# A one-core attention and expert block: route columns carried through the projection, residual by turns of x, expert weights stationary, all orders written anew

## The chip, the cores and the metric

The kernel runs on one core of a Trainium2 chip. The metric is the device time of one execution in microseconds (us). The core's engines run programs of their own and meet at semaphores: TensorE (PE) does matmuls into PSUM, VectorE (DVE) and ScalarE (ACT) do element work, GpSimd (POOL) does element work and issues the indirect DMAs, SyncE (SP) issues plain DMAs.

## What is computed

The input x has 4096 rows (4 sequences of 1024) of 128 features.

```python
x = x + attn(layernorm(x))
x = x + ffn(layernorm(x))
# attn: q, k, v = h @ W + b in 16 heads of 8; q and k normalised in each head
#       out = ((q @ k.T) / n ** sigmoid(m)) @ v ; out @ Wo + bo      (no softmax: linear)
# ffn:  logits = h @ router_w.T ; the best of 16 experts, score = sigmoid(top logit)
#       routed = (up * silu(gate)) @ down, with gate_up of the expert on h * score
#       shared = (silu(h @ sg.T) * (h @ su.T)) @ sd.T                (512 wide)
#       return shared + routed
```

Attention has no softmax, so for each sequence keys and values fold into one 128 x 128 matrix (keys times v, masked by head), which is multiplied by Wo and then applied to q.

## The kernel before, in words

**Tiling.** Rows are handled in 32 tiles of 128, four tiles to a chunk: eight chunks c = 0..7 of 512 rows. Two chunks are one sequence. Everything is float32; a float32 matmul is issued as two TensorE instructions. The shared expert's gate and up products are the exception: the operands are split into a high and a low part in float32r (`hT_hi` on ACT, `hT_lo` on POOL for the activations), and three float32r matmuls make one product.

**Stage one, attention, by chunk.** `x_stats` (L721, L724: four `bn_stats` and four `bn_aggr`), `std_x` and `x_scales` make the row scale. `project` (L1096) multiplies the columns of x (`xT`) by centred weights `w_c` into 384 columns: q, k and v. `take` (L758) scales them, adds the bias and writes `qkv` (two buffers). `square`, `head_sums` (L766), `head_norms`, `inv_norms` (L771) make the norms of the heads; POOL's `scale_v` and `scale_q` (L319) apply them. `v_by_k` (L1105) makes the 128 x 128 matrix of a sequence, `mask_vk` masks it, `fold_wo` (L1114) multiplies by Wo, `turn_q` transposes q. `attend` makes the residual in PSUM: the bias as a float32r product of 512 columns (L1129), x times the identity of 512 columns (L1130), then q times the folded matrix (L1135).

**Stage two, routing, by chunk.** ACT copies the sum out (`x1_copy`), DVE takes its statistics (`x1_stats`), `norm_h` writes `h_rows`, `turn_h` transposes them, `route` (L1152) multiplies by the router, and `choose` and `place` (ten small DVE instructions on PSUM) find each row's expert and its position `pos` in `x_slots`, a DRAM table with a region for each expert. POOL's `scatter(t)` (L345) sends one tile by an indirect DMA; it waits for the scatter two before it.

**Stage three, experts.** When all counts are known, `slot_rows` and `take_table` write a table of row numbers and expert numbers for 48 slots of 128 rows, in 12 groups of four. SP waits for all 32 scatters and loads group after group (`load`, L248: four row numbers read into registers by a TENSOR_LOAD, then four DMAs). For a group: `turn_rows` (L1215) transposes, `rows_copy` (L528), `gate_up_experts` (L1226: the rows stationary, 256 weight columns moving, the weights' address from a register), `gate` and `gated` (the score applied as a scale, one instruction per tile), `turn_act` (L1234, transposes again), `turned_act` (L877), `down_experts` (L1245), `take_y` (L545), and POOL's `send` (L354): an indirect DMA per slot into `y_back`, waiting for the send three before it.

**Stage four.** When all 48 sends have landed, SP brings `y_back` home in eight DMAs; `add_shared` and `add_experts` add, and eight DMAs write the output.

**The shared expert** is the filler. `gate_up_shared(n)` (six float32r matmuls of 512 columns, L1181 to L1183), `silu_shared(n)`, `act_shared(n)`, `down_shared(n)` (L1203) for n = 0..31, four for a chunk, stand between the other pieces in each engine's list.

**Order.** There is no scheduler: each engine's order is a written list of such calls, and an engine does the next call only when the one before has been issued. Before the first `turn_rows` TensorE does 10 of the 32 `gate_up_shared`; ACT's `score_tanh(g)` reads the score column of the loaded group g and so waits for its load.

## Time and profile before

| | us |
|---|---|
| median of 3 runs | 213.24 (212.55 to 214.74) |
| the profiled execution, whole | 212.35 |
| its span in the profile | 210.6 |
| TensorE busy | 185.7 (88%) |
| VectorE busy | 137.5 (65%) |
| GpSimd busy | 111.8 (53%) |
| ScalarE busy | 103.1 (49%) |

Times are counted from the span's start. The whole execution is 1.75 us longer than its span. TensorE's granted clock is 0.997 of full over the execution. The matmuls are pipelined, so the durations of a row overlap those of the next by some 0.15 us; the distance from start to start is what an instruction takes on the engine.

### The profile page before, as it was taken

The page shows a single profiled execution, that of the slowest core. Times are in us where ns is not written, and L with a number is a line of the kernel's source. Part 1 is how long each engine was busy: PE and PEld are TensorE (multiplying, and loading weights), DVE is VectorE, ACT ScalarE, POOL GpSimd, SP SyncE. Part 2 cuts the span into 40 slices and gives each one's busy share as a digit, 9 for nine tenths or more (in the row PEclk, how much of TensorE's full clock was granted, in tenths as well). Part 3 has the DMA queues.
Part 4 walks back from the last instruction along what each step waited for, and adds up shares of the span by engine and source line. Part 5 has one row for each costly group of instructions (what it writes and reads, how often), then busy time and mean ns, then how long its engine had stood idle before and what let it go on. Part 6 is the DMA issues. An engine that isn't in the chain of part 4 may idle for free.

```text
span 210.6 us, 3716 instructions
## 1 busy us (share of the span) xinstructions
PE 185.7 (88%) x1110; PEld 152.0 (72%) x1110; DVE 137.5 (65%) x430; ACT 103.1 (49%) x234; POOL 111.8 (53%) x142
## 2 busy tenths in 40 slices
PE   0797698988989699889779999999999999979992
PEld 0344566766668477778568999889999889869882
DVE  4789999999999979667443455454545233237553
ACT  3434474967564798943323666565634322312320
POOL 7003405348779786757800177767777767750000
PEclk9999999999999999999999999999999999999998
DMA  6999993001100011111134456511111100048143
GB/s 171 302 390 269 174 413 134 2 0 38 40 30 25 26 38 41 51 40 51 41 85 106 114 136 154 143 43 43 42 40 38 50 31 0 0 135 311 56 165 133
DMA packets 17606, 21.58 MB, mean 102 GB/s; under 512 B 3224, under 2 KB 11679, under 8 KB 17332
## 3 DMA queue, kind: packets, MB, share of 16 engines
q1 hardware_dynamic: 13872, 15.73, 26.3%
q0 software_dynamic: 2560, 4.24, 6.1%
q10 hardware_dynamic: 1156, 1.39, 1.9%
q8 instruction: 9, 0.15, 0.3%
q14 instruction: 9, 0.07, 0.1%
HBM read 13.95 MB, written 8.44 MB: 106 GB/s over the span
## 4 chain that ended last, share of the span: by engine, by line
PE 35%; DVE 31%; DMA 12%; POOL 10%; issue 8%; ACT 2%; POOLq 1%; ACTq 0%; DVEq 0%
PE quad_banks L1226 8%; DVE qkv L758 7%; DMA y_back<-yg,xg 7%; PE bank L1203 7%; POOL y_back L354 7%; DVE ss L766 4%; DVE st L721 4%; PE quad_banks L1181 3%; PE bank L1245 3%; PE quad_banks L1183 3%; PE quad_banks L1182 3%; DMA x_slots<-h_rows,pos 3%; POOL x_slots L345 2%; PE bank L1215 2%; PE quad_banks L1096 2%
## 5 line engine op out<-in xcount | busy, mean ns | idle before, releaser
L354 POOL DMA_INDIRECT y_back<-yg,xg x48 | 47.0, 979 | 30.9 <-ACT yg L545 15.2
L843 DVE TENSOR_TENSOR s_act<-quad_banks,sg_act 128x512 f32<-128x512 f32 x32 | 22.1, 689 | 28.9 <-PE bank L1203 16.6
L517 ACT ACTIVATE sg_act<-quad_banks 128x512 f32<-128x512 f32 x32 | 19.1, 598 | 44.5 <-PE quad_banks L1183 44.4
L345 POOL DMA_INDIRECT x_slots<-h_rows,pos x32 | 31.6, 988 | 11.8 <-issue 6.9
L1203 PEld LDWEIGHTS bank<-sdT,s_act 128*128 128x128 f32 x256 | 31.8, 191 | 1.8
L1203 PE MATMUL bank<-sdT,s_act 128*128 128x128 f32 x256 | 32.8, 276 | 0.0
L319 POOL TENSOR_TENSOR qkv<-qkv,rn 128x512 f32<-128x512 f32 x16 | 17.1, 1081 | 26.6 <-DVE rn L771 26.5
L1096 PE MATMUL quad_banks<-w_c,xT 128*128 128x384 f32 x64 | 25.0, 525 | 2.1 <-DVE qkv L758 1.3
L1226 PE MATMUL quad_banks<-w_gu,xgT 128*128 x96 | 22.9, 381 | 0.8 <-ACT xgT L528 0.8
L868 DVE SCALAR_TENSOR_TENSOR e_act<-quad_banks,esc,eg_act 128x128 f32<-128x128 f32 x48 | 13.5, 344 | 10.6 <-ACT eg_act L536 10.6
L1096 PEld LDWEIGHTS quad_banks<-w_c,xT 128*128 128x128 f32 x64 | 11.9, 204 | 11.0 <-issue 3.6
L1226 PEld LDWEIGHTS quad_banks<-w_gu,xgT 128*128 128x128 f32 x96 | 17.3, 190 | 2.9 <-issue 1.0
L536 ACT ACTIVATE eg_act<-quad_banks,esc 128x128 f32<-128x128 f32 x48 | 13.7, 371 | 9.3 <-PE quad_banks L1226 8.6
L758 DVE SCALAR_TENSOR_TENSOR qkv<-quad_banks,rs,b_qkv 128x384 f32<-128x384 f32 x32 | 17.6, 601 | 0.5 <-PE quad_banks L1096 0.5
L1181 PE MATMUL quad_banks<-hT,sgT 128*128 128x512 f32 x32 | 14.8, 462 | 3.3 <-DVE s_act L843 1.9
L877 DVE COPY e_actT<-bank 128x512 f32<-128x512 f32 x12 | 8.3, 690 | 13.0 <-PE bank L1234 13.0
L721 DVE BATCH_NORM_STATS2 st<-xres 128x6 f32<-128x128 f32 x64 | 13.7, 277 | 0.3 <-DMA xres<-L_attn_x 0.3
L473 ACT ACTIVATE h_rows<-xres,nm,rs 128x128 f32<-128x128 f32 x32 | 13.2, 484 | 1.0 <-DVE nm L744 1.0
L1245 PE MATMUL bank<-w_dn,e_actT 128*128 x96 | 12.7, 275 | 0.0
L1183 PE MATMUL quad_banks<-hT,sgT 128*128 128x512 f32 x32 | 12.7, 395 | 0.0
L1182 PE MATMUL quad_banks<-hT,suT 128*128 128x512 f32 x32 | 12.7, 395 | 0.0
L1245 PEld LDWEIGHTS bank<-w_dn,e_actT 128*128 128x128 f32 x96 | 12.3, 191 | 0.5
(141 smaller groups left out, 348.0 us busy)
## 6 DMA issues: line engine op xcount, KB each, us to landing
xg<-x_slots SPq DMA_DIRECT2D x48, 65.0 KB, 1.9
xT<-x_t SPq DMA_DIRECT2D x8, 256.0 KB, 7.1
xres<-L_attn_x SPq DMA_DIRECT2D x8, 256.0 KB, 7.2
w_gu<-gate_up SPq DMA_DIRECT2D x1, 2048.0 KB, 14.4
h_rows<-y_back SPq DMA_DIRECT2D x8, 256.0 KB, 5.4
x_slots<-zeros SPq DMA_DIRECT2D x1, 1040.0 KB, 16.4
w_dn<-down SPq DMA_DIRECT2D x1, 1024.0 KB, 16.4
out<-xres SPq DMA_DIRECT2D x4, 256.0 KB, 2.0
```

The costliest lines, as they stand in the source:

```text
L345: g.indirect_dma_start(out=x_slots, out_offset=bass.IndirectOffsetOnAxis(ap=pos[:, t:t + 1], axis=0), in_=h_rows[:, t, :], in_offset=None) ...
L354: nc.gpsimd.indirect_dma_start(out=y_back, out_offset=bass.IndirectOffsetOnAxis(ap=xg[:, n, D + 1:D + 2].bitcast(I32), axis=0), in_=yg[:, ...
L517: a.activation(sg_act[:, n % 2], pair[:, 2 * (n % 2)], ACT.Silu).then_inc(s_silu, 1)
L721: last = v.bn_stats(st[:, t, :], xres[:, t, :])
L758: last = v.scalar_tensor_tensor(out=qkv[:, c % QRING, j, :], in0=pair[:, j, 0:QKV], scalar=rs1[:, t:t + 1], in1=b_qkv[:], op0=ALU.mult, op ...
L843: v.tensor_tensor(s_act[:, n % 2], pair[:, 2 * (n % 2) + 1], sg_act[:, n % 2], ALU.mult).then_inc(s_act_rdy, 1)
L1096: last = te.matmul(pair[:, j, 0:QKV], xT[:, P * (Q * c + j):P * (Q * c + j + 1)], w_c[:], start=True, stop=True)
L1181: te.matmul(to, lhs[:, 0], rhs[:, 0], start=True, stop=False)
L1182: te.matmul(to, lhs[:, 0], rhs[:, 1], start=False, stop=False)
L1203: last = te.matmul(Y_BANK[c][:, here], s_act[:, n % 2, here], sdT[:, D * k:D * k + D], start=(k == 0 and j == 0), stop=(k == KC - 1 and j ...
L1226: mm = te.matmul(gate_up_banks(g % 2)[:, j, :], xgT[:, g % 2, P * j:P * j + P], gu_cols[:, bass.ds(held[g][j] * 2, F2)], start=True, stop= ...
L1245: mm = te.matmul(ps_yg[:, here], e_actT[:, g % 2, here], dn_cols[:, bass.ds(cols[j], D)], start=True, stop=True)
```

## The change

**Projection.** The value columns leave it; the router's 16 columns enter: 272 columns for 384. `keep` (DVE) holds the router columns. `gram` multiplies scaled keys by the raw rows of x (and two added columns for the mean and the bias) in place of keys by v; per sequence a transpose `turn_g`, a copy `gT_copy` and a product `v_of_g` with Wv come in before the mask. The folded matrix gets 16 more columns, so that `attend` also gives the attention's part of the route logits; `route` is gone, and `sum_logits` adds the two parts. The router's choice no longer waits for the normalised rows.

**Residual.** `bias_x` (ACT) adds bo to the columns of x, and `attend` transposes these 128 x 128 pieces into PSUM in place of the bias product and the identity product. It works in halves of two tiles, and so does `x1_copy` (288 columns).

**Statistics.** `bn_stats` runs over two interleaved tiles at once (its even and odd halves are the two tiles); `bn_aggr` is gone.

**Choice.** The small instructions of `choose` and `place` are functions of their own, on SBUF tiles of two buffers, put between other work. Inverse norms of k get a factor more (`scale_inv`).

**Experts.** The score is multiplied onto the loaded rows (`scale_rows`, DVE). ACT copies the four experts' weights of a group to `w_now` (`take_weights`), which is stationary; the rows move, 128 columns at a time, so the gate and up come out transposed: `turn_act` and `turned_act` are gone, and `gate` and `gated` are one instruction of 512 columns each.

**Splitting.** `hT_lo` of chunks 0 to 3 is on DVE, of 4 to 7 on POOL, all ahead of the sends.

**Orders.** All lists are new. 13 `gate_up_shared` stand before the first `turn_rows`.

```diff
-        Y_BANK = [bank[n] for n in (1, 0, 0, 1, 0, 1, 0, 1)]
+        Y_BANK = [bank[n] for n in (3, 3, 3, 3, 3, 3, 3, 3)]
...
-                    last = te.matmul(pair[:, j, 0:QKV], xT[:, P * (Q * c + j):P * (Q * c + j + 1)], w_c[:], start=True,
+                    last = te.matmul(pair[:, j, 0:PROJ], xT[:, P * (Q * c + j):P * (Q * c + j + 1)], w_c[:, 0:PROJ],
...
-                te.matmul(ps_qy[:], ones_r[:], bo_two[:].rearrange("p j d -> p (j d)"), start=True, stop=False)
-                te.matmul(ps_qy[:], ident[:], xres[:, Q * c:Q * c + Q, :].rearrange("p j d -> p (j d)"), start=False,
+                for j in (0, 1):
+                    te.matmul(ps_y[:, YW * j:YW * j + D], xT_b[:, c % XRING, P * (2 * h + j):P * (2 * h + j + 1)], ident[:],
+                              start=(j == 0), stop=False, is_transpose=True, skip_group_check=True)
...
+            def take_weights(g):
+                if g == 0:
+                    act.wait_ge(table_rdy, 1)
+                    act.wait_ge(ld_wg, 16)
+                first = slot_values(1, g, mybir.EngineType.Activation, (E - 1) * D)
+                if g >= 2:
+                    act.wait_ge(e_gu_mm, g - 1)
+                for j in range(Q):
+                    last = a.copy(w_now[:, (g * Q + j) % WRING], gu_cols[:, bass.ds(first[j] * 2, F2)])
+                last.then_inc(w_rdy, 1)
...
+            def scale_rows(g):
+                dve.wait_ge(esc_rdy, g + 1)
+                here = slice(g * Q, g * Q + Q)
+                rows = xg[:, here, 0:D]
+                v.tensor_tensor(rows, rows, esc[:, here].unsqueeze(2).broadcast_to([P, Q, D]), ALU.mult).then_inc(xg_rdy, 1)
...
+            def sum_logits(c):
+                dve.wait_ge(x1_rdy, 2 * c + 2)
+                dve.wait_ge(kept_rdy, c + 1)
+                mark(("lg", c), v.tensor_tensor(lg[:, c % 2], x1[:, quad(c), D:YW], kept[:, c], ALU.add))
...
+            def stats(c, rows, st, done):
+                for n in (0, 1):
+                    last = v.bn_stats(st[:, 2 * c + n, :], by_two(rows, Q * c + 2 * n))
+                last.then_inc(done, 1)
...
+            down_shared(28, after=(fin, 7))
```

The last line means that the last chunk's down products wait until seven chunks are finished, the experts' part included.

The order on ACT at the opening of the expert stage before. `half_tanh` is a group's score (it needs that group's load), `xgT` the copy of its transposed rows, `eg_act` its gate, `yg` its result for POOL.

```order
L522 ACTIVATE half_tanh<-xg 128x4
L528 COPY xgT<-bank3 128x512
L536 ACTIVATE eg_act<-quad_banks,esc 128x128 x4
L522 ACTIVATE half_tanh<-xg 128x4
L528 COPY xgT<-bank3 128x512
L536 ACTIVATE eg_act<-quad_banks,esc 128x128 x4
L522 ACTIVATE half_tanh<-xg 128x4
L545 COPY yg<-bank2 128x512
```

The same place on ACT in the changed kernel, up to the weights of group 2 (`sg_act` is the shared expert's).

```order
L602 ACTIVATE half_tanh<-xg 128x4
L597 ACTIVATE sg_act<-quad_banks 128x512
L602 ACTIVATE half_tanh<-xg 128x4
L608 COPY xgT<-bank0 128x512
L602 ACTIVATE half_tanh<-xg 128x4
L597 ACTIVATE sg_act<-quad_banks 128x512
L602 ACTIVATE half_tanh<-xg 128x4
L625 ACTIVATE eg_act<-quad_banks 128x512
L608 COPY xgT<-bank0 128x512
L602 ACTIVATE half_tanh<-xg 128x4
L244 TENSOR_LOAD table
```

Before, three scores stand ahead of the first result (`yg`); now four stand ahead of the first gate, and two more, with a group's weights between them, ahead of the first result (`hT_full` is then its place):

```order
L618 ISA
L618 COPY w_now<-w_gu 128x256
L602 ACTIVATE half_tanh<-xg 128x4
L636 COPY hT_full<-bank1 128x512
L608 COPY xgT<-bank0 128x512
```

So the first send to `y_back` is behind the load of group 5, where it was behind that of group 2.

The order on DVE at chunk 3's choice, before (all on PSUM, in one run):

```order
L791 TENSOR_REDUCE h_rows<-bank 128x4
L792 TENSOR_TENSOR bank<-bank,h_rows 128x64
L793 SCALAR_TENSOR_TENSOR bank<-bank,place_of 128x64
L795 TENSOR_REDUCE near<-bank 128x4
L796 TENSOR_TENSOR hot<-bank,near 128x4x16
L800 SCALAR_TENSOR_TENSOR incl<-run_mask,hot 128x64
```

And in the changed kernel, with the tiles in SBUF and other work between:

```order
L948 TENSOR_TENSOR lg<-x,kept 128x64
L862 BN_STATS st<-x 128x6 x2
L952 TENSOR_REDUCE top<-lg 128x4
L930 TENSOR_SCALAR gs<-bank 128x128
L956 TENSOR_TENSOR far<-lg,top 128x64
L960 SCALAR_TENSOR_TENSOR far<-far,place_of 128x64
L880 RECIPROCAL rs<-sd 128x4
L965 TENSOR_REDUCE near<-far 128x4
L983 TENSOR_TENSOR h_rows<-top,rs 128x4
L913 TENSOR_REDUCE ss<-sq 128x128
L906 TENSOR_TENSOR kept<-quad_banks,b_log 128x64
```

The same choice is now spread between the statistics, the sums of the next heads and the logits kept, and several of its instructions read two SBUF tiles where one operand was in PSUM.

## Rows read from the trace of the kernel before

**Rows 1.** The page's part 1: busy us (share of the span) xinstructions
```profile
PE 185.7 (88%) x1110; PEld 152.0 (72%) x1110; DVE 137.5 (65%) x430; ACT 103.1 (49%) x234; POOL 111.8 (53%) x142
```
**Rows 2.** Timeline of POOL: start us, us, what (first and last scatter, first and last send)
```profile
46.67 1.19 POOL L345 DMA_INDIRECT x_slots<-h_rows,pos  x1 [0.63 <-issue]
...
101.95 0.96 POOL L345 DMA_INDIRECT x_slots<-h_rows,pos  x1 [0.31 <-issue]
...
120.39 1.01 POOL L354 DMA_INDIRECT y_back<-yg,xg  x1 [14.94 <-ACT yg L545]
...
183.67 0.98 POOL L354 DMA_INDIRECT y_back<-yg,xg  x1 [0.30 <-issue]
```
**Rows 3.** Timelines of SP from 105 to 108 and to 120, and from 183 on, merged
```profile
105.79 1.91 SPq L248 DMA_DIRECT2D xg<-x_slots  x4
...
105.79 14.27 SPq L248 DMA_DIRECT2D xg<-x_slots  x24
...
185.85 4.68 SPq L254 DMA_DIRECT2D h_rows<-y_back  x8
```
**Rows 4.** The page's part 6: issues, KB each, us from issue to landing
```profile
xg<-x_slots SPq DMA_DIRECT2D x48, 65.0 KB, 1.9
...
h_rows<-y_back SPq DMA_DIRECT2D x8, 256.0 KB, 5.4
```
**Rows 5.** Timeline of PE, attention (projection; bias, identity, q product; route)
```profile
8.00 7.34 PE L1096 MATMUL quad_banks<-w_c,xT 128*128 128x384 f32 x16 [0.66 <-ACT w_c L451]
...
53.33 2.75 PE L1096 MATMUL quad_banks<-w_c,xT 128*128 128x384 f32 x8
...
61.23 0.48 PE L1129 MATMUL bank<-bo_two,ones_r 128*128 128x512 f32 x1
61.55 1.02 PE L1130 MATMUL bank<-xres,ident 128*128 128x512 f32 x2
62.41 1.05 PE L1135 MATMUL bank<-wb,qT 128*128 128x128 f32 x8
...
64.86 0.96 PE L1152 MATMUL bank<-rwT,hT_full 128*128 128x16 f32 x8
```
**Rows 6.** The chain that ended last: start us, us, what (experts, then the shared tail)
```profile
118.08 0.89 PE bank L1245 x8
118.98 1.73 PE quad_banks L1226 x8
120.71 0.44 PE bank L1234 x4
...
187.67 0.89 PE bank L1203 x8
189.96 0.89 PE bank L1203 x8
...
207.43 0.69 DVE xres L855
```
**Rows 7.** The groups view, DVE and ACT: busy, mean ns of one | idle before
```profile
L758 DVE SCALAR_TENSOR_TENSOR qkv<-quad_banks,rs,b_qkv 128x384 f32<-128x384 f32 x32 | 17.6, 601 | 0.5 <-PE quad_banks L1096 0.5
...
L721 DVE BATCH_NORM_STATS2 st<-xres 128x6 f32<-128x128 f32 x64 | 13.7, 277 | 0.3 <-DMA xres<-L_attn_x 0.3
...
L528 ACT COPY xgT<-bank 128x512 f32<-128x512 f32 x12 | 7.2, 597 | 8.6 <-PE bank L1215 8.6
...
L724 DVE BATCH_NORM_AGGREGATE mv<-st 128x2 f32<-128x6 f32 x64 | 6.1, 157 | 0.6
...
L517 ACT ACT_TABLE_LOAD x2 | 2.6, 1283 | 0.0
...
L792 DVE TENSOR_TENSOR bank<-bank,h_rows 128x64 f32<-128x64 f32 x8 | 1.9, 233 | 0.3
```
**Rows 8.** Timelines of DVE and of POOL, the same moments
```profile
64.58 2.27 DVE L784 TENSOR_TENSOR suT<-w_sh,suT 128x512 fp32r<-128x512 f32 x1
...
65.00 1.29 POOL L329 TENSOR_TENSOR hT<-hT_full,hT 128x512 fp32r<-128x512 f32 x1
```

1617 lines of the change are left out of this document (943 added, 674 removed).

## The prediction

> **What bounds the kernel now.** I read the page's busy line first, then the chain that ended last, the timelines of GpSimd and SyncE, and the groups view. TensorE is busy 88% of the span [rows 1]: 24.9 us of 210.6 are idle. In the expert stage the chain shows it without a gap: a down product at 118.08, the next group's gate and up at 118.98, the transposes at 120.71 [rows 6]. So it looks like TensorE's kernel. But a second chain runs beside it. GpSimd issues 32 scatters, the first at 46.67 and the last at 101.95; after that come the loads of the slots, and then 48 sends from 120.39 to 183.67, one every 1.3 us [rows 2]. SyncE's loads start at 105.79, 3.84 after the last scatter's start; 4 issues take 1.9 us and 24 take 14.3, some 0.6 each [rows 3], and each lands 1.9 after its issue [rows 4]. Only after the last send come the loads of `y_back`, from 185.85 to 190.5 [rows 3], landing 5.4 later [rows 4], that is by 195.5, 11.8 after the last send's start. Before the change this second chain is some 10 us ahead at the end: TensorE's last products end near 206.5, just ahead of the two last additions, the second at 207.43 [rows 6]. A change that shortens TensorE's work by more than 10 us hands the end to the second chain, and this one touches what that chain waits for.
>
> **What TensorE loses.** By starts, as matmuls overlap. Projection: 8 instructions of 384 columns in 2.75 us [rows 5], 0.32 each without the overlap, 64 of them 20.5 us; with 272 columns 14.5: 6.0 saved. Residual: from the bias product at 61.23 to the q product at 62.41 [rows 5] are 1.18, eight times 9.4; now 32 transposes at 0.11 (four in 0.44 [rows 6]), 3.5, and 16 more columns on 64 instructions, 0.6: 5.3 saved. Route: 0.96 less the overlap, 0.8, eight times: 6.5 saved. `turn_act`: 12 times 0.44 [rows 6]: 5.3 saved. Added: `turn_g`, `v_of_g` and the longer first products, some 24 instructions of at most 0.11: 1.8 with the first ones slow. The experts' gate and up: 8 instructions of 256 columns took 1.73; now 16 of 128, which cost 0.11 each by the down product (8 in 0.89 [rows 6]), 1.78: 12 times 0.05, 0.6. Sum: 23.1 - 2.4 = 20.7 us less work. The bounds of what it gives are 0 and 20.7.
>
> **The opening is later.** ScalarE now copies x plus bias and takes a square root ahead of `w_c`; its operand `wo_all` is the fourth of its DMAs. Estimate: a wait of some 1, a copy of 0.6 [rows 7] twice, one table load of 1.28 [rows 7]: about 3 us, so `project` starts at 11 and not at 8.00 [rows 5]. VectorE does statistics meanwhile, so not all of it is lost.
>
> **VectorE up to the first placement.** Ten `stats` calls: 4 x 0.277 + 4 x 0.157 [rows 7] is 1.7 busy, some 1.2 by starts; now two instructions on 256 elements, which no row shows: between 2 x 0.277 (no gain from pairing is lost) and 4 x 0.277. I take 0.7, nearer the first, as 0.277 holds a fixed part: 5.0 saved. Ten `take` of two instructions, 0.601 at 384 columns [rows 7], some 0.46 at 256: 2.7 saved. The bias rows 1.8 and one `inv_norms` 0.9 saved. Against that `keep`, `scale_inv`, `gram_out`, an earlier `weights_lo`, and eight more instructions of a choice at about 0.23 [rows 7]: some 6. Net -4.5, and +3 for the opening, and at its head VectorE also waits some 3 for products that come late. That alone is +1.5; two inputs from SBUF (below) add up to 3. I take the first scatter 3 us later, 49.7, between -1 and +4.
>
> **GpSimd to the last scatter.** The same 32 scatters and 16 scalings. Two splits (1.29 each [rows 8]) leave the run, one enters: -1.3. So the last scatter starts at 101.95 + 3 - 1.3 = 103.7. It can't be much earlier, since the run is paced by itself; it can be later if positions come late: the last two chunks' residuals now stand behind five `gate_up_shared`, and ScalarE makes 9 table loads where it made 5, 1.28 each [rows 7], two of them straight ahead of the last chunk's statistics. Bounds: 99.5 and 109.5.
>
> **The loads, and the scores ahead of the first gate.** A group g lands at last scatter + 3.8 + 0.6 (4g + 3) + 1.9, group 5 by +19.7 (24 issues in 14.3 [rows 3]). Before, three scores stood ahead of the first result; now `score_tanh(5)` does. So the first result is copied at +19.9 and sent from +20.6, where it was +18.4: 124.3. That TensorE has four transposes less in this stretch is worth nothing there. Cost 2.2. Taking the weights costs ScalarE 48 copies of 256 columns, at most 0.6 each and by columns 0.3 [rows 7]: 14 to 29 us of a stage of 60, hidden while the sends set the pace.
>
> **The sends.** 47 distances took 63.3; one held a split of 1.3 and its issue: 61.8 without. But all twelve scores stand ahead of `gate(3)`, group 11 lands near +35, and the tenth send wants group 3's result, at +38, while by pace it is due at +34. A starvation of 0 to 5 us; I take 1.5, since any faster load takes all of it away. Last send: 124.3 + 61.8 + 1.5 = 187.6, which is 3.9 later than before.
>
> **The end.** Loads landed 11.8 later, 199.4. Then one addition of the experts and one of the shared part, 0.6 each by starts; `down_shared(28)` waited for them (`fin, 7`), and four down products of 0.89 [rows 6] follow, 3.6; an addition of 0.69, and the output, which took 2.5 from the last addition's end at 208.12 [rows 6] to the span's end: 8.2 in all. 199.4 + 8.2 = 207.6. TensorE's own route: first rows turned at 103.7 + 7.4 + 1.2 (score and `scale_rows`) = 112.3; then 19 shared gate-ups of 1.40 (2.29 less 0.89 [rows 6]), 22 downs of 0.89, and 12 groups of 0.44 + 1.78 + 0.89: 83.6, which ends at 195.9, the span at 199.2; with the same score waits, up to 7.7, at 206.9. Both routes meet near 207. The execution is 1.75 longer than its span: 207.6 + 1.75 = 209.4, against 212.35 of the profiled execution (-1.4%) and 213.24 of the median (-1.8%).
>
> **A rule that speaks against it.** VectorE's split of a weight took 2.27 us, from 64.58 to 66.85, while GpSimd's multiplication ran from 65.00 to 66.29 [rows 8]; an instruction of the same size with two SBUF inputs took 0.69 at 207.43 [rows 6], with GpSimd idle. The Trainium skill (SBUF — State Buffer, section SBUF: two separate sides) says that a VectorE instruction with two SBUF inputs and a GpSimd instruction that reads SBUF exclude each other for the whole instruction. By that rule, the trace agrees. It matters as the choice moves from PSUM to SBUF.
>
> **The rivals.** (1) TensorE's saving counts in full and the scores don't bind: 199.2 + 1.75 = 201. For it: TensorE's chain without gaps [rows 6]. Against: the loads' pace [rows 3] is the same code as before. (2) Slower: the choices and `scale_inv` meet GpSimd's eight scalings, of the split's size, in the middle of the scatter run, each costing VectorE some 0.7 (half of a split's 1.29 [rows 8]), 5.6 in all; the positions of chunk 4 come after GpSimd has run dry, and the last scatter starts at 109.5, 5.8 later: 215.2. It decides from a last scatter at 109 on. For it: the 2.27 us, and a VectorE without idle time in the first 70 us (0.5 us of it before all `take` [rows 7]). Against: the small instructions are short, and more of them fall beside scatters than beside scalings; no row shows a scatter holding one up. (3) No change: one us more on the scatters and 2 more of starvation: 212.4. For it: both were sized in the middle of their bounds.
>
> **How the numbers follow.** My forecast has 0.42, rival 1 0.12, rival 2 0.22, rival 3 0.24. Within 1% (210.2 to 214.5) is about what a measurement of this kernel can't tell from no change. The forecast lies faster in 0.35 of its 0.42, with rival 1 0.47; same: 0.07 and 0.20 of rival 3, 0.27; slower: rival 2 and the rest of rival 3, 0.26. Range: from 201.5, close to rival 1, to 216.5, beyond rival 2's 215.2; the likeliest case's own range is 206 to 212.5.
>
> **What would show it.** Right: the first scatter at 48 to 51, the last at 102 to 106, the first send 20 to 21 after the last scatter and waiting for `yg`, with ScalarE's score waiting for the load of `xg`; a gap before the tenth to twelfth send; the last down products waiting for VectorE. TensorE busy near 165. Wrong: sends that start less than 18 after the last scatter, or a last scatter before 100; then it is nearer 201. A last scatter after 108, with GpSimd idle near 80 and long two-input instructions on VectorE: rival 2.

## The result, and the profile after

The changed kernel takes 228.0 us (median of 4 runs, 227.6 to 229.7), the kernel before 213.65 beside it: a ratio of 1.069, with an interval of 1.061 to 1.077. It is slower by some 14 us, outside the range of the prediction. The profiled execution took 227.85 us with a span of 226.1.

The page's busy line of the changed kernel, against [rows 1]:

```profile
PE 176.1 (78%) x1120; PEld 152.6 (67%) x1120; DVE 133.2 (59%) x345; ACT 124.2 (55%) x270; POOL 108.4 (48%) x138
```

TensorE has less to do, and its idle time has doubled: 50 us of the span, where it was 25. GpSimd is busy 3.4 us less than before, in a span 15.5 us longer. So the places to look at are the four of [rows 2], in the timeline of POOL (start us, us, engine, line, operation, idle time before and what ended it):

```profile
49.65 1.18 POOL L370 DMA_INDIRECT x_slots<-h_rows,pos  x1 [3.76 <-DVE pos L1001]
...
87.39 0.22 POOL L359 TENSOR_TENSOR seen<-seen,incl 128x16 bf16<-128x16 bf16 x1 [3.21 <-DVE incl L977]
89.60 1.01 POOL L370 DMA_INDIRECT x_slots<-h_rows,pos  x1 [1.99 <-DVE h_rows L983]
...
113.76 0.96 POOL L370 DMA_INDIRECT x_slots<-h_rows,pos  x1 [0.30 <-issue]
...
134.64 1.01 POOL L378 DMA_INDIRECT y_back<-hT_full,xg  x1 [15.93 <-ACT hT_full L636]
...
151.69 0.98 POOL L378 DMA_INDIRECT y_back<-hT_full,xg  x1 [1.53 <-DMA y_back<-hT_full,xg]
...
181.13 0.98 POOL L378 DMA_INDIRECT y_back<-hT_full,xg  x1 [0.30 <-issue]
182.41 0.98 POOL L378 DMA_INDIRECT y_back<-hT_full,xg  x1 [0.30 <-issue]
185.31 0.98 POOL L378 DMA_INDIRECT y_back<-hT_full,xg  x1 [1.93 <-DMA y_back<-hT_full,xg]
...
204.44 0.98 POOL L378 DMA_INDIRECT y_back<-hT_full,xg  x1 [0.30 <-issue]
```

These starts cut the span into five stretches. The table has them for the kernel before, as predicted, and for the changed kernel, and then for the runs below, so that each can be read against its own stretch (c2, c4 and c5 are c3 with the edit of e7, e9 and e10). All are starts of one profiled execution each.

| us | to first scatter | run of scatters | last scatter to first send | sends | last send to end | span |
|---|---|---|---|---|---|---|
| before | 46.7 | 55.3 | 18.4 | 63.3 | 26.9 | 210.6 |
| predicted | 49.7 | 54.0 | 20.6 | 63.3 | 20.0 | 207.6 |
| changed | 49.7 | 64.1 | 20.9 | 69.8 | 21.7 | 226.1 |
| e1 order of sends | 50.5 | 63.3 | 21.2 | 65.3 | 20.4 | 220.7 |
| e2 choice in PSUM | 50.1 | 60.5 | 21.5 | 68.8 | 20.7 | 221.6 |
| e3 shared first | 50.7 | 62.6 | 20.0 | 70.3 | 20.7 | 224.3 |
| e4 scores late | 50.5 | 64.3 | 17.7 | 67.1 | 20.4 | 219.9 |
| e5 opening | 47.7 | 63.5 | 21.6 | 68.5 | 21.0 | 222.2 |
| e6 chunk 4's positions | 49.6 | 63.9 | 21.5 | 69.1 | 22.7 | 226.8 |
| e7 chunks 6, 7 first | 50.6 | 71.2 | 20.6 | 70.4 | 22.4 | 235.1 |
| e8 e6 and e7 | 50.1 | 70.7 | 21.9 | 71.6 | 21.1 | 235.4 |
| e9 e8, split moved | 50.4 | 62.1 | 27.1 | 71.7 | 20.6 | 231.8 |
| e10 e6, chunk 6 first | 50.4 | 64.9 | 20.4 | 70.1 | 20.7 | 226.5 |
| b1 before, changed sends | 47.5 | 55.2 | 18.4 | 69.1 | 28.6 | 218.8 |
| b2 before, choice in SBUF | 48.2 | 56.5 | 18.5 | 63.4 | 26.9 | 213.5 |
| c1 six edits | 46.6 | 60.1 | 18.3 | 62.7 | 21.8 | 209.5 |
| c3 c1 and the last sums | 47.3 | 60.0 | 18.4 | 64.1 | 18.2 | 208.1 |
| c2 c3 and e7 | 47.7 | 66.6 | 18.9 | 62.6 | 19.0 | 214.9 |
| c4 c3 and e9 | 46.1 | 58.7 | 26.0 | 62.3 | 19.3 | 212.3 |
| c5 c3 and e10 | 47.2 | 61.2 | 18.1 | 64.2 | 18.6 | 209.3 |

The prediction is right in three of the five stretches, within 2 us. The miss is in two: the run of scatters, 10.1 us longer than predicted, and the sends, 6.5 longer. Kernels that do the same up to there have their first scatter anywhere from 49.6 to 50.7, so nothing should be read from a difference of some 1 us in one stretch.

The run of scatters has two halves that behave differently. Scatter 16 is the first of chunk 4 (in the changed kernel the one at 89.60). "Predicted" is the kernel before, less the two splits that left the first half, plus the one that entered the second.

| us | first scatter to scatter 16 | scatter 16 to last |
|---|---|---|
| before | 33.3 | 22.0 |
| predicted | 30.7 | 23.3 |
| changed | 39.9 | 24.2 |
| e2 choice in PSUM | 36.5 | 24.0 |
| e6 chunk 4's positions | 35.3 | 28.6 |
| c1 six edits | 30.7 | 29.4 |

So 9.2 of the 10.1 us that the run of scatters is too long stand ahead of scatter 16. In e1, e3, e4 and e5, which change nothing between these two scatters, the first half takes 39.2 to 40.3 us, so the smaller numbers of e2, e6 and c1 are clear of chance.

What GpSimd waited for in the run of scatters stands in its view of waits, from 40 to 116 us (engine, what, who it waited for: us, times, longest):

```profile
POOL seen L359 <- DVE incl L977: 7.9, 4, 3.2
POOL x_slots L370 <- DVE pos L1001: 6.6, 3, 3.8
POOL x_slots L370 <- DMA x_slots<-h_rows,pos: 5.7, 7, 2.2
POOL x_slots L370 <- issue: 5.3, 21, 0.3
...
POOL x_slots L370 <- DVE h_rows L983: 2.0, 1, 2.0
```

And of the kernel before, from 40 to 103:

```profile
POOL x_slots L345 <- issue: 6.9, 24, 0.7
POOL x_slots L345 <- DMA x_slots<-h_rows,pos: 3.4, 5, 1.7
...
POOL seen L336 <- DVE incl L800: 1.6, 1, 1.6
POOL x_slots L345 <- DVE pos L811: 1.4, 2, 0.9
```

Waits for VectorE's positions, counts and scores are 16.5 us where they were 3.0; 6.5 of the 16.5 lie ahead of the first scatter (the 3.76 above, and a count's 2.69 at 45.63). Landings of earlier scatters are 2.3 us more. So GpSimd isn't slower: up to scatter 16 VectorE brings the positions late. Behind it, this kernel's scatters wait for earlier scatters to land and for nothing else but their own issue. The largest wait is for chunk 4: scatter 16 at 89.60, after GpSimd had stood still in three pieces since scatter 15: 0.94 at 81.45, and the two rows above.

### The profile page after: what moved, and what is told of

Its sections match the earlier page's. It is cut to its first block, busy times and chain, and to the rows that moved or that the text cites. A ratio compares the mean times of both kernels' runs of the same rounds, so it can differ in the third digit from the quotient of the medians.

```text
span 226.1 us, 3737 instructions
## 1 busy us (share of the span) xinstructions
PE 176.1 (78%) x1120; PEld 152.6 (67%) x1120; DVE 133.2 (59%) x345; ACT 124.2 (55%) x270; POOL 108.4 (48%) x138
## 3 DMA queue, kind: packets, MB, share of 16 engines
q10 hardware_dynamic: 1152, 1.65, 2.2%
## 4 chain that ended last, share of the span: by engine, by line
PE 23%; DVE 20%; issue 15%; POOL 13%; DMA 13%; SPq 11%; ACT 3%; ACTq 0%; POOLq 0%; DVEq 0%
SPq L271 9%; POOL y_back L378 6%; PE quad_banks L1425 6%; POOL x_slots L370 5%; PE quad_banks L1557 4%; DVE qk L898 3%; PE bank L1537 3%; DMA x_slots<-h_rows,pos 3%; DMA m_col<-m_of_column 3%; DMA h_rows<-y_back 3%; DMA y_back<-hT_full,xg 3%; PE bank L1570 3%; DVE rn L918 2%; DVE st L862 2%; SPq L244 1%
## 5 line engine op out<-in xcount | busy, mean ns | idle before, releaser
L378 POOL DMA_INDIRECT y_back<-hT_full,xg x48 | 47.9, 997 | 38.9 <-ACT hT_full L636 18.2
L1033 DVE TENSOR_TENSOR s_act<-quad_banks,sg_act 128x512 f32<-128x512 f32 x32 | 21.9, 688 | 28.6 <-ACT sg_act L597 28.5
L342 POOL TENSOR_TENSOR qk<-qk,rn 128x512 f32<-128x512 f32 x16 | 17.7, 1113 | 29.6 <-DVE rn L918 29.3
L1425 PE MATMUL quad_banks<-w_c,xT 128*128 128x272 f32 x64 | 21.6, 482 | 6.9 <-ACT w_c L511 5.0
L1557 PE MATMUL quad_banks<-xgT,w_now 128*128 128x128 f32 x192 | 24.1, 282 | 1.9 <-issue 1.9
L1557 PEld LDWEIGHTS quad_banks<-xgT,w_now 128*128 128x128 f32 x192 | 23.1, 197 | 2.7 <-issue 2.4
L1512 PE MATMUL quad_banks<-hT,sgT 128*128 128x512 f32 x32 | 15.5, 483 | 4.1 <-DVE s_act L1033 4.1
L1570 PE MATMUL bank<-w_dn,e_act 128*128 x96 | 14.3, 297 | 4.4 <-DVE e_act L1077 4.4
L618 ACT COPY w_now<-w_gu 128x256 f32 x48 | 15.9, 406 | 2.6 <-PE quad_banks L1557 1.3
L898 DVE SCALAR_TENSOR_TENSOR qk<-quad_banks,rs,b_all 128x256 f32<-128x256 f32 x32 | 13.8, 473 | 4.3 <-PE quad_banks L1425 4.3
L542 ACT ACTIVATE h_rows<-x,nm,rs 128x128 f32<-128x128 f32 x32 | 13.2, 484 | 2.3 <-DVE nm L884 2.1
L1514 PE MATMUL quad_banks<-hT,sgT 128*128 128x512 f32 x32 | 13.1, 409 | 0.0
L1513 PE MATMUL quad_banks<-hT,sgT 128*128 128x512 f32 x32 | 13.1, 408 | 0.0
```

Of the source, the lines that this page charges most:

```text
L378: g.indirect_dma_start(out=y_back, out_offset=bass.IndirectOffsetOnAxis(ap=xg[:, n, D + 1:D + 2].bitcast(I32), axis=0), in_=yg[:, n // Q % ...
L898: last = v.scalar_tensor_tensor(out=qk[:, c % QRING, j, :], in0=pair[:, j, 0:QK], scalar=rs1[:, t:t + 1], in1=b_all[:, 0:QK], op0=ALU.mult ...
L1033: v.tensor_tensor(s_act[:, n % SRING], pair[:, 2 * (n % 2) + 1], sg_act[:, n % 2], ALU.mult).then_inc(s_act_rdy, 1)
L1425: last = te.matmul(pair[:, j, 0:PROJ], xT[:, P * (Q * c + j):P * (Q * c + j + 1)], w_c[:, 0:PROJ], start=True, stop=True)
L1512: te.matmul(to, lhs[:, 0], rhs[:, 0], start=True, stop=False)
L1514: return te.matmul(to, lhs[:, 1], rhs[:, 0], start=False, stop=True)
```

## The experiments

Times are medians. A ratio is to the kernel before, timed beside it; the changed kernel's own is 1.069 (1.061 to 1.077).

**e1, the order of the sends.** The changed kernel's sends go 6, 8, 9, 7, 12, 10, 11, 13, and so on; each waits for the send with a number three lower.

```diff
-send_one(6) send_one(8) send_one(9) send_one(7) send_one(12) ...
+send_one(6) send_one(7) send_one(8) send_one(9) send_one(10) ...
```

> The changed kernel with GpSimd's 48 sends in the plain order 0, 1, ... 47. Theory S (the order of the sends): each send waits for the send three before it by number; in the changed order (6, 8, 9, 7, 12, 10, ...) some wait for a send issued only two places earlier, 2 x 1.28 us, and the extra gaps before sends 8, 9, 12, 13, 28, 32, 33, 40, 44 and 45 add to about 6.4 us. Then the last send goes from 204.4 to about 198.5 and the time falls by 5 to 6.5 us, to about 222. Theory L (the sends wait because the rows or the landings are late, whatever the order): the same waits appear before the sends in plain order, and the time moves by less than 1.5 us.

Measured: 224.1 us, ratio 1.049 (1.042 to 1.056); the sends take 65.3 us in place of 69.8. Theory S, though less than it expected (3.9 us of time, where it had 5 to 6.5). The rows above show how it works: send 33, at 185.31, waits for send 30, at 181.13, which in this order is only two places ahead. Two places are 2 x 1.28 = 2.6 us, and from 181.13 to 185.31 are 4.2; in plain order the room is 3.8. A wait remains at the same places in plain order, but a smaller one: GpSimd's waits for landings and issue are 15.2 us in e1 and 20.7 in the changed kernel.

**b1, the same order in the kernel before.**

```diff
-send(0) ... send(9) hT_lo(5) send(10) send(11)
+send_one(0) ... send_one(6) send_one(8) send_one(9) send_one(7) send_one(12) ... hT_lo(5) ...
```

> The kernel before with the changed kernel's order of the 48 sends (6, 8, 9, 7, 12, 10, 11, 13, ...; the split of chunk 5 on GpSimd stands behind the same 40 sends). Theory S (the order itself costs, by waits for a send only two places earlier): the last send goes 4 to 6 us later than 183.7 and the time rises by 4 to 6 us, to about 218.5. Rival L (the order does nothing by itself, and the changed kernel's sends wait for rows that are late there): less than 1.5 us.

Measured: 220.8 us, ratio 1.031 (1.025 to 1.037). The sends take 69.1 us where they took 63.3, as in the changed kernel. So the order alone costs 5.8 us of sends, with rows that are early. That all of it arrives at the end has a second cause, which I hadn't priced. (The time rises by 3.1%, 6.6 us.) The timeline of PE in b1:

```profile
183.23 0.79 PE L1216 MATMUL quad_banks<-hT,sgT 128*128 128x512 f32 x1 [7.11 <-POOL hT L329]
```

TensorE stands still for 7.1 us, because GpSimd's split of chunk 5 is queued behind 40 sends. The two chains of the kernel before, which I had called independent with 10 us between them, are tied there.

**e2, the tiles of the choice in PSUM.**

```diff
-lg[:, c % 2], far[:, c % 2], offs[:, c % 2], rank[:, c % 2]
+columns of ps_s (bank 3) for chunks 0 to 5; down_shared(0) waits for pos_rdy 6
```

> The changed kernel with the tiles of the choice (lg, far, offs, rank) of chunks 0 to 5 in PSUM bank 3, which is free until the first shared down product, in place of SBUF. Theory P (VectorE instructions with two SBUF inputs stand still while GpSimd scales q or k): the held instructions L1001 (1.34 us), L960 (1.48) and L993 (1.74) fall to 0.2 each, VectorE gains some 4 us before chunk 4, the last scatter comes 3 to 4 us earlier than 113.8, and the time falls by 2.5 to 4 us, to about 225; L983, L948 and L1038, which still read two SBUF tiles, stay held where they meet a scaling. Theory O (the run of scatters is late through the order alone: positions of chunk 4 queued behind the work of chunk 5): last scatter and time within 1 us of the changed kernel.

Measured: 225.7 us, ratio 1.057 (1.050 to 1.064), the run of scatters 60.5 us in place of 64.1, the last scatter at 110.6 in place of 113.8. By the stretch it is theory P, with a little less at the end than expected; the interval of the time touches the changed kernel's, so the time alone wouldn't tell. Timeline of DVE in the changed kernel (both inputs in SBUF):

```profile
53.30 1.34 DVE L1001 TENSOR_TENSOR pos<-rank,near 128x4 int32<-128x4 f32 x1
...
56.77 1.48 DVE L960 SCALAR_TENSOR_TENSOR far<-far,place_of 128x64 f32<-128x64 f32 x1
...
58.76 1.71 DVE L983 TENSOR_TENSOR h_rows<-top,rs 128x4 f32<-128x4 f32 x1
...
62.28 1.81 DVE L993 TENSOR_TENSOR offs<-offs,hot 128x64 f32<-128x64 f32 x1
```

and of POOL at the same moments:

```profile
53.53 1.08 POOL L342 TENSOR_TENSOR qk<-qk,rn 128x512 f32<-128x512 f32 x1
...
57.08 1.08 POOL L342 TENSOR_TENSOR qk<-qk,rn 128x512 f32<-128x512 f32 x1
...
59.36 1.08 POOL L342 TENSOR_TENSOR qk<-qk,rn 128x512 f32<-128x512 f32 x1
...
62.90 1.09 POOL L342 TENSOR_TENSOR qk<-qk,rn 128x512 f32<-128x512 f32 x1
```

Each VectorE instruction ends within 0.1 us of the scaling's end (53.30 + 1.34 = 54.64 against 54.61). A multiplication of 128 x 4 elements took 1.71 us, as long as it had to stand behind the scaling; free of one it takes 0.16. In each of the four pairs VectorE's start is recorded before the scaling's, by 0.2 to 0.6 us, and yet VectorE is the one that stands; these rows don't show what decides who goes first. Over the first half of the run six small instructions are held so, 7.6 us beyond what they take alone (the four above, 75.69 and 79.49). The splits of chunks 2 and 3, which the change put on VectorE, meet two scalings as well, 2.86 us for two that take 1.29 elsewhere:

```profile
81.87 2.86 DVE L1038 TENSOR_TENSOR hT<-hT_full,hT 128x512 fp32r<-128x512 f32 x2
```

In e2 the line of own_only, now with a PSUM input (shortest, median and longest in ns, first and last start), and the timeline of DVE at the first scaling of the run and at the same two splits:

```profile
L1009 DVE TENSOR_TENSOR bank<-bank,hot x6: 216/222/232, 48.4 to 85.5; 128x64 f32<-128x64 f32 x6
```

```profile
53.97 1.20 DVE L964 TENSOR_TENSOR bank<-x,kept 128x64 f32<-128x64 f32 x1
...
76.75 5.03 DVE L1054 TENSOR_TENSOR hT<-hT_full,hT 128x512 fp32r<-128x512 f32 x2
```

The six instructions are no longer held (216 to 232 ns, where one had 1.81 us), but the next one with two SBUF inputs, the sum of the logits, is held in their place (1.20), and the two splits now stand behind three scalings in a row, 5.03 us for 1.3 of work. So moving a tile takes away only the meetings it can't pass on, and e2's 3.6 us are less than what the holds cost.

**b2, the choice in SBUF in the kernel before.**

```diff
-def far_of(c): return log_bank(c)[:, 192:192 + Q * E]...   (also offs_of, rank_of)
+def far_of(c): return far_sb[:]
```

> The kernel before with far, offs and rank of all chunks in SBUF in place of PSUM. Theory P (two SBUF inputs on VectorE against GpSimd's scalings and splits): some of its L793, L796, L809 and L811 (0.23 to 0.27 us each) take 0.8 to 1.6 us where they meet one, 2 to 4 us in all, and the last scatter comes 1 to 3 us later than 101.95. At the end little of it arrives, since in this kernel the sends end some 10 us before TensorE: within 1.5 us. Rival (the holds in the changed kernel come from something else): all of these stay below 0.5 us.

Measured: 215.65 us, ratio 1.009 (1.004 to 1.014); last scatter 104.7 in place of 101.95, of which 1.5 is there at the first scatter. The groups view:

```profile
L812 DVE TENSOR_TENSOR offs_sb<-offs_sb,hot 128x64 f32<-128x64 f32 x8 | 4.2, 529 | 0.3
...
L796 DVE SCALAR_TENSOR_TENSOR far_sb<-far_sb,place_of 128x64 f32<-128x64 f32 x8 | 3.0, 374 | 0.3
```

529 and 374 ns, where the same two had 232 and 233: 3.5 us more in sixteen instructions. Theory P, in the other direction. At the end 0.9% arrived, 1.9 us, with an interval from 0.8 to 3.1 that holds the 1.5 I had set as a limit; the time doesn't say more.

**e3, the shared sums first.**

```diff
-SHARED_FIRST = [0, 1, 2, 3, 4, 5]        down_shared(28, after=(fin, 7))
+SHARED_FIRST = [0, 1, 2, 3, 4, 5, 6, 7]  down_shared(28, after=(y_free, 7))
```

> The changed kernel with chunks 6 and 7 treated as the other six: their shared sum is added before the returned rows land, so that the last four shared down products wait for nothing of the returned rows. Theory T (the tail holds 3.8 us of down products and a 0.7 us sum between the last load and the output): the time falls by 4 to 5 us, to about 223.5, with the last send where it was (204.4). Rival: the end is set by something else (the loads and outputs of the other chunks, or TensorE, which still has the products to do): less than 1.5 us.

Measured: 226.8 us, ratio 1.059 (1.050 to 1.068), not told apart from the changed kernel. Theory T missed, and the rival is in the trace. Timeline of DVE in e3:

```profile
215.68 0.69 DVE L1045 TENSOR_TENSOR x<-bank,x 128x512 f32<-128x512 f32 x1 [2.25 <-PE bank L1537]
216.29 4.89 DVE L1057 TENSOR_TENSOR hT_full<-x,h_rows 128x512 f32<-128x512 f32 x8
```

The last sum of the shared part waits for TensorE's products to 215.7, not for the returned rows. TensorE's list and the sends end within 1 us of each other, and taking one away shows the other. Part of it was my order: all eight additions, 4.9 us, stood behind that last sum, as the row shows.

**e4, the scores late.**

```diff
 gate(0) rows_copy(1)
-score_tanh(4) take_weights(2) score_tanh(5) take_y(0) ...
-take_y(2) score_tanh(8) score_tanh(9) score_tanh(10) score_tanh(11) gate(3)
+take_weights(2) take_y(0) score_tanh(4) ...
+take_y(2) gate(3) ... score_tanh(11)
```

> The changed kernel with ScalarE's score_tanh(4) to (11) and VectorE's scorings each about two groups ahead of their use, in place of five ahead of the first take_y and four in a row ahead of gate(3). Theory A (only the first send is behind a score wait; GpSimd's queue sets the path from there): TensorE's pause near 141 to 148 goes, the first send comes 1.5 to 2.5 us earlier than 134.6, and the time falls by 1.5 to 2.5 us, to about 226. Theory B (the pause before gate(3) starves the sends, as the prediction had it at 1.5 and up to 5 us): 4 us or more. If neither, within 1 us.

Measured: 223.5 us, ratio 1.048 (1.039 to 1.056). The first send comes 17.7 us after the last scatter, below the kernel before's 18.4, and the sends take 2.7 us less too. The time fell by 4.5 us, so it is theory B in size and both in mechanism. In the changed kernel the timeline of ACT reads:

```profile
144.47 0.21 ACT L602 ACTIVATE half_tanh<-xg 128x4 f32<-128x4 f32 x1 [1.90 <-DMA xg<-x_slots]
147.09 0.21 ACT L602 ACTIVATE half_tanh<-xg 128x4 f32<-128x4 f32 x1 [2.40 <-DMA xg<-x_slots]
147.20 0.58 ACT L625 ACTIVATE eg_act<-quad_banks 128x512 f32<-128x512 f32 x1
```

and that of PE, and the chain that ended last:

```profile
148.64 1.65 PE L1570 MATMUL bank<-w_dn,e_act 128*128 x8 [2.42 <-DVE e_act L1077]
```

```profile
145.00 2.07 DMA xg<-x_slots
...
181.13 3.11 DMA y_back<-hT_full,xg
```

The gate of group 3 goes at 147.20, the moment the last rows of group 11 are there. In e4 it goes earlier, though its rows come later by a us:

```profile
141.46 0.60 ACT L625 ACTIVATE eg_act<-quad_banks 128x512 f32<-128x512 f32 x1 [1.67 <-PE quad_banks L1557]
```

5.7 us earlier. The chain of the changed kernel runs from the last loads over gate 3 and TensorE to send 28 at 175.55, which waited 0.81 us for its rows, and on over the sends: the pause before gate 3 came back as late rows there.

The pause was paid for a second time. TensorE had stood still from 146.2 to 148.6, and was granted half its clock from about 148.9 to 152.4. The window's row has the us, then busy us and instructions of PE, PEld, DVE, ACT and POOL, then PEclk, the granted clock (1.00 is 2.4 GHz, 0.50 is 1.2), DMA share and GB/s:

```profile
148.90:152.40 3.50, 3.50 (x16) 3.21 (x16) 1.10 (x2) 2.25 (x5) 1.97 (x2) 0.53 0.09 31
```

The eight down products at 148.64 took 1.65 us where the same eight take 0.89 at the full clock, and they are on the chain that ended last. Some 1.6 us went that way by estimate, (1 - 0.53) x 3.5; in e4 the clock is 1.00 from 140 to 160.

**e5, the opening.**

```diff
-w_first, b_all, m_col, wo_all        bias_x(0) x_std(0) bias_x(1) wc_copy()
+m_col, w_first, b_all, wo_all        wc_copy() x_std(0) bias_x(0) x_std(1) bias_x(1)
```

> The changed kernel with m_col as the first of ScalarE's four loads and the copy of w_c ahead of the first biased x and the first square root. Theory V (VectorE is busy from its first statistics to the positions of chunk 4, so that what the opening gains arrives at the first scatter and goes on to the end): the first projection starts at 8.5 to 9 us in place of 12.9, the first scatter comes at 46 to 47.5 in place of 49.7 to 50.7, and the time falls by 3 to 4 us, to about 224.5. Rival (later steps are paced by something else, the loads of x or GpSimd's scalings, and eat the gain): less than 1.5 us at the end though the first projection moved.

Measured: 224.4 us, ratio 1.048 (1.042 to 1.055). Theory V in the time; the steps on the way are smaller than expected (the projection at 10.2, not 8.5 to 9). The timeline of ACT in the changed kernel, and that of PE in the changed kernel and in e5:

```profile
8.60 0.29 ACT L502 ACTIVATE m_tmp<-m_col,zero_col 128x1 f32<-128x1 f32 x1 [4.49 <-DMA m_col<-m_of_column]
```

```profile
12.87 3.63 PE L1425 MATMUL quad_banks<-w_c,xT 128*128 128x272 f32 x8 [5.04 <-ACT w_c L511]
```

```profile
10.16 3.99 PE L1425 MATMUL quad_banks<-w_c,xT 128*128 128x272 f32 x8 [0.58 <-ACT w_c L511]
```

0.5 KB of `m_col`, third in ScalarE's queue, held ScalarE and VectorE to 8.60. With it first, the projection starts 2.7 us earlier and waits 0.58 us for `w_c` in place of 5.04, and the first scatter 2.0 earlier. The rest of the 4 us at the end is not in one stretch (0.6 in the run, 1.3 in the sends), and I don't read it as shown.

**e6, chunk 4's positions.**

```diff
-act_shared(0) hT_lo(2) hT_lo(3) [choice of 5] add_base(4) ... put(4)      count(5) scatter(16)
+hT_lo(2) add_base(4) ... put(4) act_shared(0) hT_lo(3) [choice of 5]      scatter(16) ... count(5)
```

> The changed kernel with VectorE's add_base(4) to put(4) right behind the split of chunk 2, in place of behind the whole choice of chunk 5, and GpSimd's count(5) behind scatter(19). Theory O (the positions of chunk 4 are late through the written order): scatter 16 goes at 85.5 to 87 in place of 89.6 us, the last scatter comes 2.5 to 3.5 us earlier than 113.8, and the time falls by 2 to 3.5 us. Rival (scatters from there wait for landings, or chunks 6 and 7 are as late as before): last scatter and time within 1 us.

Measured: 229.3 us, ratio 1.067 (1.057 to 1.077): nothing. Scatter 16 did move, as the timeline of POOL shows:

```profile
84.88 1.00 POOL L370 DMA_INDIRECT x_slots<-h_rows,pos  x1 [0.86 <-DVE pos L1001]
...
99.46 0.21 POOL L359 TENSOR_TENSOR seen<-seen,incl 128x16 bf16<-128x16 bf16 x1 [3.22 <-DVE incl L977]
...
102.46 0.96 POOL L370 DMA_INDIRECT x_slots<-h_rows,pos  x1 [1.65 <-ACT h_rows L542]
```

4.7 us earlier than 89.60, and all of it was given back at chunk 6: the count waits 3.2 us and the scatter behind it 1.7 for ScalarE's norm. Chunk 4 was a limit, but not the last one. Part of the 4.7 us is a hold too: with the splits of chunks 2 and 3 apart, the two take 1.35 us together and not 2.86. With e2's and e6's edits together (c1), the first half of the run takes 30.7 us, as predicted.

**e7 and e8, chunks 6 and 7 ahead of the shared work** (e8 with e6's edit).

```diff
-silu(2) x1_copy(6, 0) silu(3) x1_copy(6, 1) h_std(6) silu(4) ... silu(6) norm_h(7) silu(7)
+x1_copy(6, 0) x1_copy(6, 1) x1_copy(7, 0) h_std(6) x1_copy(7, 1) norm_h(6) h_std(7) norm_h(7) silu(2) ... silu(7)
```

(TensorE's and VectorE's orders likewise.)

> The changed kernel with the residual, the norm and the choice of chunks 6 and 7 ahead of the shared experts' gates 3 to 7 on TensorE, ScalarE and VectorE (four table loads of 1.28 us fewer on ScalarE before the norm of chunk 7). Theory R (the end of the run of scatters is set by chunks 6 and 7, whose statistics stand behind the shared gates and their table loads): rows and positions of chunk 7 are there some 4 us earlier, the last scatter starts at 111 to 112 in place of 113.8, limited from there by chunk 4's start at 89.6 and the pace of 1.3 us; time 1.5 to 2.5 us less. Rival: the landings of the scatters pace the run; last scatter within 1 us.

> The changed kernel with e6's edit and e7's together. Theory R with O (chunk 4 and chunks 6 and 7 are two limits one behind the other, so that e6 alone gave nothing): the last scatter starts at 106.5 to 109 us and the time falls by 4 to 6.5 us, to about 222.5, more than the two alone add to. Rival (another limit, landings or GpSimd itself): no more than e7 alone.

Measured: 235.6 and 236.2 us, ratios 1.098 (1.089 to 1.106) and 1.101 (1.093 to 1.108). Both are slower, and theory R isn't tested by them, since my order made two new waits. The timeline of POOL in e7, and the row of the window from 100 to 110 us (columns as above):

```profile
109.49 0.96 POOL L370 DMA_INDIRECT x_slots<-h_rows,pos  x1 [0.30 <-issue]
119.05 1.26 POOL L352 TENSOR_TENSOR hT<-hT_full,hT 128x512 fp32r<-128x512 f32 x1 [8.61 <-ACT hT L554]
```

```profile
100.00:110.00 10.00, 5.07 (x14) 3.97 (x15) 4.67 (x18) 4.87 (x10) 6.90 (x10) 0.54 0.14 47
```

GpSimd's split of chunk 4 stands between scatter 29 and 30, and its input now comes behind six silus: 8.6 us of stillness. And TensorE, with its shared work pushed back, was busy half of the window and was granted 0.54 of its clock, so near the lower of its two levels, 1.2 GHz; in the changed kernel the same window has 8.1 us busy and 1.00.

**e9, the split behind the scatters** (on top of e8).

```diff
-scatter(29) hT_lo(4) scatter(30) scatter(31)      norm_h(7) silu_shared(2) silu_shared(3)
+scatter(29) scatter(30) scatter(31) hT_lo(4)      silu_shared(2) silu_shared(3) norm_h(7)
```

> e8_both with GpSimd's split of chunk 4 behind scatter(31) and ScalarE's silus 2 and 3 ahead of the norm of chunk 7. In e7_residual_first GpSimd stood still for 8.6 us at that split, between scatter 29 (109.5) and scatter 30 (120.5). Theory R with O (chunk 4's positions and then chunks 6 and 7 set the run of scatters): last scatter at 106.5 to 109 in place of 113.8. If landings of the scatters pace it: 111 to 113. The time: the shared experts' work is some 10 us later on TensorE (its share and clock fell between 100 and 110 in e7), so little of the gain can arrive; 222 to 230.

Measured: 233.5 us, ratio 1.094 (1.085 to 1.102). The last scatter is at 112.4, so 1.4 us earlier and not 5 to 7: R with O falls in this form. The number lies in the rival's 111 to 113, that landings pace the run, but the trace doesn't bear it out: behind the first scatter GpSimd waits 11.6 us for VectorE and 4.0 for landings. And the first send is 27 us after it, since VectorE's table of the slots, started at 115.80 where it was at 106.94, stands behind its `act_shared(2)` to `(6)`, which wait for the shared work that was pushed back.

**e10, chunk 6 alone ahead** (on top of e6).

```diff
-silu(2) x1_copy(6, 0) silu(3) x1_copy(6, 1) h_std(6)
+x1_copy(6, 0) x1_copy(6, 1) h_std(6) silu(2) silu(3)
```

> e6_pos4 with both halves of chunk 6's residual ahead of shared gate 3, ScalarE's square root of chunk 6 ahead of silu 2 (two table loads fewer), and the shared work otherwise kept between chunks 6 and 7. Theory R with O (positions of 4, then chunk 6 and 7, limit the run): count(6) no longer waits 3.2 us, the last scatter starts at 109 to 111.5 in place of 113.5, and the time falls by 2 to 4 us against the changed kernel's 228.0. Rival (the chunk 7 chain of products, copies and one table load per change of function takes as long as before): last scatter within 1 us, or the table later as in e9, and the time 228 or more.

Measured: 229.0 us, ratio 1.078 (1.064 to 1.091), last scatter at 115.3: the rival. I haven't found an order that shortens chunks 6 and 7.

**c1, c3 and the other combinations.** c1 has the edits of e1 to e6; c3 also puts seven of the eight last additions ahead of the last shared sum; c2, c4 and c5 are c3 with e7's, e9's and e10's edits.

> The changed kernel with all six edits: plain order of sends, choice tiles in PSUM, shared sums first, late scores, the opening, chunk 4's positions. If the waits found so far are what the change lost by and they stand one behind the other on the path (first scatter, run of scatters, first send, sends, tail), the gains add: 4 of the sends, 3 of the tiles, 4.5 of the tail (TensorE no longer at the end, since the score wait is gone), 2.5 of the scores, 3.5 of the opening, 2.5 of the positions, 20 in all from 228, so 206 to 211 us, below the kernel before (213.7). If they overlap, 212 to 218.

> c1_all with VectorE's additions of returned chunks 0 to 6 ahead of the last shared sum. TensorE sets the end in c1_all (last down products end near 200.9, then eight additions in 4.9 us): 2.5 to 3 us less, about 209.5, 2.5% below the kernel before. If the last loads of the returned rows, which land near 199, set it instead: 1 us or less.

Measured: c1 212.2 us, ratio 0.991 (0.987 to 0.994); c3 210.3, ratio 0.986 (0.982 to 0.991). c3 beats both kernels; it and c1 aren't told apart. Of the 20 us that I added up for c1, 16 arrived. The sends gave 7.1 where I had 4, and the last stretch nothing where I had 4.5 (21.8 us, before 21.7). There the end is TensorE's list, as e3 points to and the timelines of PE and DVE in c3 show:

```profile
198.54 3.73 PE L1555 MATMUL bank<-sdT,s_act 128*128 128x128 f32 x32
```

```profile
199.97 4.29 DVE L1073 TENSOR_TENSOR hT_full<-x,h_rows 128x512 f32<-128x512 f32 x7
204.18 0.69 DVE L1061 TENSOR_TENSOR x<-bank,x 128x512 f32<-128x512 f32 x1
```

The last down products end at 202.3, and the last sum starts only at 204.18, since seven additions queue ahead of it.

> c1_all with e7's edit and with VectorE's additions of returned chunks 0 to 6 ahead of the last shared sum. In c1_all TensorE's last down products end near 200.9 us, then eight additions take 4.9 and the output follows: the end is TensorE's. Expected: the additions save 2.5 to 3.5 us of the 4.9, the earlier chunks 6 and 7 another 1 to 3 where TensorE's idle time before the experts shrinks with them: 206 to 209 us, 2 to 3.5% below the kernel before. If TensorE's work is no shorter by the earlier scatters, 209 to 210.

> c3 with e9's edit of chunks 6 and 7 and of the split. If the scatters come 3 us earlier (last near 103.5 in place of 106.7) and TensorE, whose list sets the end, isn't delayed: 206 to 208. If TensorE is delayed by the shared work that now comes later, as in e7: 211 to 215, slower than c3.

> c3 with e10's edit of chunk 6. If the scatters come 2 us earlier and TensorE is not delayed, 208 to 209.5; if it is delayed, 210 to 213, no better than c3's 210.3.

Measured: c2 217.4 (1.017, 1.010 to 1.023), c4 213.8 (1.006, 1.002 to 1.010), c5 211.1 (0.993, 0.988 to 0.997). As alone, so in the combination: e7's and e9's orders cost time; e10's gives nothing.

## Why the prediction was wrong, step by step

- **What TensorE loses.** The residual was right: at 75.80 to 76.44 the changed kernel does half a chunk in 0.64 us, so 1.3 a chunk, where 2.07 stood before (1.18 and 0.89): 6.3 us saved, predicted 5.3. The projection was right too, at the full clock: eight instructions of 272 columns take 1.83 us from start to start there, 0.229 each (0.227 predicted), and 3.63, 0.454 each, where half the clock was granted:

```profile
25.03:28.66 3.63, 3.63 (x10) 2.70 (x10) 2.62 (x8) 1.03 (x4) 2.08 (x3) 0.50 1.13 286
31.38:33.21 1.83, 1.83 (x10) 1.47 (x9) 1.83 (x4) 1.72 (x4) 0.00 (x0) 1.00 0.93 394
```

- **TensorE's clock: a term put at nothing.** The prediction takes every TensorE duration from a kernel with a granted clock of 0.997 and doesn't ask what more idle time does to it. The changed kernel had 0.955: TensorE stood still from 19.8 to 24.2, 63.9 to 65.8, 132.5 to 134.4 and 146.2 to 148.6, and during each of these pauses or soon after it a stretch of 3 to 7 us at 0.50 began. (Not with every pause: 2.3 us before 60.7 had none.) By estimate this is (1 - 0.955) x 226.1 = 10.2 us of lost clock, and most of it shows as busy time: TensorE busy "near 165" came out at 176.1. What it cost the time is shown only for the stretch behind gate 3 (e4).
- **The opening.** Predicted at 11, measured 12.87. What I missed was `m_col`, which moved from first to third in the queue, landed 6.8 us after its issue and held VectorE to 8.9. I had looked only at `wo_all`.
- **VectorE up to the first placement.** First scatter 49.7 predicted, 49.65 measured. The pair of statistics took 0.67 by starts (predicted 0.7), a `take` instruction 0.473 (0.46). The opening was 1.9 us later than predicted, so something else was as much smaller, which no run tells apart: the match is partly luck.
- **GpSimd to the last scatter: the first step that failed.** I wrote "it can't be much earlier, since the run is paced by itself" and gave 103.7 with an upper bound of 109.5; it was 113.8. The run isn't paced by itself here: 10.0 us of its waits are for VectorE (the 16.5 less the 6.5 ahead of the first scatter). The sum has no term at all for VectorE behind the first placement, though the change put four splits and the longer choices there, on an engine with hardly any idle time (9.5 of 10 us busy from 40 to 90). Rival 2 had the mechanism right, and its signs appeared (GpSimd idle between 79 and 90, long two-input instructions); e2 and b2 show it. It sized it at 5.6 us; the held small instructions alone are 7.6 and the two splits 1.6. "The small instructions are short, and more of them fall beside scatters than beside scalings" is false where VectorE has no idle time, since one that meets a scaling pays for all of what is left of it, and when it is let go the next scaling is near. e2 takes back 3.6 us of the 10.1. That chunk 4's positions stand behind chunk 5's choice is the other cause (e6 moves scatter 16 by 4.7 us). With both edits, in c1, the half of the run up to scatter 16 is at the 30.7 us of the prediction, and the holds there are down to some 2 us (two instructions of 0.2 us took 1.2 and 1.3): so these two are what its 9.2 us were (of c1's other edits, the opening alone leaves 39.4 there, e5, and the rest come later). What they give isn't kept. With chunk 4 early, chunks 5, 6 and 7 are the limit, and the second half grows from 24.2 to 29.4: GpSimd waits 3.5 us for chunk 6's count, 2.7 for ScalarE's normalised rows, 2.2 for chunk 5's. What would shorten it stays open, since e7, e9 and e10 each made another wait. No run put the four splits back on GpSimd.
- **The loads, and the scores ahead of the first gate.** 20.6 predicted, 20.9 measured, and e4, which puts the scores behind, brings 17.7. This step was right in place, and in size within 1 us.
- **The sends: the second step that failed.** I took 61.8 us of pace from the kernel before, and 1.5 of starvation. The pace isn't a property of GpSimd: it holds as long as each send has three places to land in. The changed order breaks that, which I could have read from the new list beside the wait in `send_one`, and costs 4.5 us (e1) to 5.8 (b1). The starvation before gate 3 was there as described (the last rows at +33.3, predicted near +35), but its price wasn't 1.5: with e4 the sends alone fall by 2.7 us, part of it by the clock. The two add: 4.5 and 2.7 from 69.8 are 62.6, and c1, with both, is at 62.7 (c3, with the same sends, at 64.1).
- **The end.** 11.8 + 8.2 = 20.0 predicted, 21.7 measured. The last load landed at 216.4, 11.95 us after the last send (predicted 11.8). From there to the first of the last products at 219.10 are 2.7 us, where the sum had 1.2: three additions of the experts and one of the shared part stood ahead of it, and I had counted one of each. The last products did wait for them. The products, the last sum and the output took 3.82, 0.69 and 2.5 us, where the sum had 3.6, 0.69 and 2.5 (with the 1.2 these are 8.0, not the 8.2 that it states). That TensorE's own route and the sends meet at the end was right too, and is why e3 gave so little.
- **What bounds the kernel now.** "The second chain is some 10 us ahead at the end" was wrong as a margin. b1 delays the last send by 6.5 us, and the time rises by as much (3.1%, 6.6 us), because the splits of chunks 5 to 7 are in the same queue. A chain that ends early isn't free if others stand in its queue.

The stretches add up: 3.0 + 8.8 + 2.4 + 6.5 - 5.3 = 15.4 us, the 15.5 between the spans but for rounding. As far as these runs show, the work that the change takes from TensorE is worth only the last term and what c3 shows: with the orders mended, the same arithmetic is 1.4% faster than the kernel before (0.982 to 0.991).
